# First spectral product in 64x64 blocks with the transform in quarters; behind the expert loop nested conditions, and the own rows of two images added by GpSimd

## The reference, cut to what matters

```python
o1r = relu(einsum(xr, w1[0]) - einsum(xi, w1[1]) + b1[0])   # per block of 24 channels
o1i = relu(einsum(xi, w1[0]) + einsum(xr, w1[1]) + b1[1])
o2r = softshrink(einsum(o1r, w2[0]) - einsum(o1i, w2[1]) + b2[0])
o2i = softshrink(einsum(o1i, w2[0]) + einsum(o1r, w2[1]) + b2[1])
x = irfft2(o2r + 1j * o2i) + x
t = t + attention(layernorm(t))
n = layernorm(t)
t = t + shared(n) + sum over two experts e of comb[:, e] * expert_e(n)
```

## Time and profile before

| | |
|---|---|
| median of 3 runs | 228.53 us |
| the profiled execution's own time | 227.28 us |
| its span, first to last instruction | 225.4 us |
| TensorE matmuls busy | 217.2 us (96%) |
| TensorE weight loads | 140.8 us (62%) |
| VectorE | 148.7 us (66%) |
| ScalarE | 113.8 us (50%) |
| GpSimd | 77.2 us (34%) |

### The profile page before, as it was taken

How to read it: one execution, slowest core, us unless ns; L and a number is a source line. 1 busy time by engine, 2 the same in 40 slices (tenths; PEclk the granted TensorE clock), 3 DMA queues, 4 the chain that set the end, 5 groups by cost and what they waited for, 6 DMA issues and landing times.

```text
span 225.4 us, 5766 instructions
## 1 busy us (share of the span) xinstructions
PE 217.2 (96%) x1975; PEld 140.8 (62%) x1975; DVE 148.7 (66%) x353; ACT 113.8 (50%) x205; POOL 77.2 (34%) x119
## 2 busy tenths in 40 slices
PE   7999999999999999999999999999999999897994
PEld 3988866765676676767755745655556565453393
DVE  3558767677878888787879756666566666560262
ACT  0742274555444444345643567566575766653271
POOL 7040052000001811837101626566565666442100
PEclk9999999999999999999999999999999999999999
DMA  6973564939989979015600211111211111210444
GB/s 179 184 186 88 153 237 102 292 75 354 287 165 292 244 200 286 0 38 171 198 20 0 52 34 52 52 42 52 52 52 48 52 40 52 55 35 22 146 153 140
DMA packets 28115, 27.53 MB, mean 122 GB/s; under 512 B 7804, under 2 KB 26940, under 8 KB 28092
## 3 DMA queue, kind: packets, MB, share of 16 engines
q1 hardware_dynamic: 22444, 21.15, 34.0%
q0 software_dynamic: 2304, 4.72, 7.5%
q10 hardware_dynamic: 3344, 1.36, 2.3%
HBM read 22.34 MB, written 3.44 MB: 114 GB/s over the span
## 4 chain that ended last, share of the span: by engine, by line
PE 88%; DVE 5%; ACT 3%; issue 2%
PE grid L1624 11%; PE bank L1650 10%; PE grid L1365 8%; PE grid L1631 7%; PE bank L1640 4%; PE bank L1385 4%; PE bank L1227 4%; PE grid L1511 3%; PE grid L1335 3%; PE bank L1402 3%; PE bank L1335 2%; PE bank L1287 2%; PE bank L1350 2%; PE grid L1525 2%; PE bank L1193 2%
## 5 line engine op out<-in xcount | busy, mean ns | idle before, releaser
L1110 DVE COPY main<-main 128x1152 f32 x39 | 30.3, 790 | 15.2 <-issue 13.6
L776 ACT ACTIVATE main<-down_all 128x576 f32 x40 | 27.2, 684 | 25.6 <-PE bank L1650 24.7
L742 ACT ACTIVATE main<-grid 128x1024 f32<-128x1024 f32 x23 | 23.6, 1025 | 26.3 <-PE grid L1365 26.3
L589 POOL DMA_INDIRECT main<-xhat_rows,main x21 | 26.9, 1282 | 24.4 <-PE bank L1610 13.4
L597 POOL DMA_INDIRECT pair_rows<-main x19 | 20.2, 1061 | 25.6 <-DVE main L1100 25.6
L1624 PE MATMUL grid<-main 128*64 128x384 f32 x152 | 28.2, 488 | 0.6 <-DVE main L1094 0.6
L1335 PE MATMUL grid<-main 32*128 32x256 f32 x132 | 27.1, 401 | 0.0
L1365 PE MATMUL grid<-main 32*128 32x256 f32 x192 | 26.3, 398 | 0.8 <-ACT main L742 0.6
L913 DVE TENSOR_REDUCE main<-grid 128x2 f32<-128x512 f32 x33 | 21.8, 685 | 4.4 <-PE grid L1335 3.6
L1650 PEld LDWEIGHTS bank<-main 128*64 128x64 f32 x228 | 16.1, 136 | 12.4 <-ACT main L776 8.9
L1650 PE MATMUL bank<-main 128*64 128x192 f32 x228 | 22.7, 333 | 0.0
(11 more groups left out here) (221 smaller groups left out, 395.3 us busy)
## 6 DMA issues: line engine op xcount, KB each, us to landing
down_all<-wd SPq DMA_DIRECT2D x4, 1152.0 KB, 7.0
main<-wg SPq DMA_DIRECT2D x4, 576.0 KB, 4.6
main<-wu SPq DMA_DIRECT2D x4, 576.0 KB, 6.1
main<-wg SPq DMA_DIRECT2D x4, 288.0 KB, 6.8
main<-wu SPq DMA_DIRECT2D x4, 288.0 KB, 8.0
main<-main SPq DMA_DIRECT2D x8, 128.0 KB, 3.6
main<-x SPq DMA_DIRECT2D x1, 768.0 KB, 7.5
main<-wg SPq DMA_DIRECT2D x2, 384.0 KB, 5.7
```

The source lines that it names most:

```text
L589: pool.indirect_dma_start(xg[:, t % 2, :], None, xhat_rows, bass.IndirectOffsetOnAxis(ap=slot_token[:, t:t + 1].bitcast(U32), axis=0)).the ...
L742: act.activation(probs[:, quad % 2, 2 * (n % 2):2 * (n % 2) + 2, :, :].rearrange("p h k n -> p h (k n)"), grid[:, score_banks(n), :], ACT. ...
L776: act.activation(w_dn[:, p, h, :], dn_e(expert(t, h)), ACT.Copy).then_inc(S["w_dn_ready"], 1)
L1110: vec.tensor_copy(w_gu[:, p, h, :], gu_e(expert(t, h))).then_inc(S["w_gu_ready"], 1)
```

## The change

It has three parts.

1. *The start.* `spec`, `hid`, `w1` and `w2` get a new layout of the 128 partitions: quarters of 32, real and imaginary part of one block of 24 channels, then of another. The transform (L1179) has 16 matmuls a unit with 32 output columns in place of 8 with 64. The first layer has 16 matmuls of 64x64 weights in place of 8 of 128x128, in steps of four that lie on the four quadrants of the array and go to two banks. Its evictions are shared: ScalarE takes one of the two banks (relu with bias), VectorE the other (add the bias, then the maximum with 0), counted by the new semaphore `hid_dve`; a step of the second pair of images waits for the evictions of the same step of the first pair. VectorE negates in two instructions of 32 partitions, that of `w2` in front of its third eviction. All of `w2` is loaded by SyncE, `b1` by four loads of ScalarE in place of two, and `w_proj` with its bias before `w_qkv`, the gate's loads (new semaphore `ld_gate`) behind it. The spreading to `w_first` stands behind L993.
2. *The loop.* `loop_pairs` reads the number of pairs before the loop. Pairs 8 to 11 stand unrolled, each in a condition inside the body of the one before.
3. *The tail.* For tiles 0 to 3 GpSimd adds the own rows to the first share, between `first_share` and `mix` (new semaphore `own_ready`). TensorE no longer transposes own rows of images 0 and 1. It does both parts of `shared_down` first, then the routed rows of all images, then the own rows of images 2 and 3. VectorE mixes two tiles in place of three before the last hidden product.

```diff
@@ -321,17 +322,20 @@
+            pairs = engine.value_load(used_i[0:1, 1:2], min_val=SURE // 2, max_val=TILES // 2)
...
-            pairs = engine.value_load(used_i[0:1, 1:2], min_val=SURE // 2, max_val=TILES // 2)
-            with engine.Fori(SURE // 2, PAIRS - 1) as i:
+            def further(i):
                 with engine.If(pairs > i):
                     step(2 * i, 0, i)
                     step(2 * i + 1, 1, i)
-            with engine.If(pairs > PAIRS - 1):
-                for t in range(TILES - 3, TILES - 1):
-                    step(t, t % 2, t // 2)
+                    if i + 1 < PAIRS:
+                        further(i + 1)
+            further(SURE // 2)
...
@@ -410,14 +414,21 @@
-        def load_blocks(queue, dst, src, sem, k):
-            i, o = slice(BLK * k, BLK * k + BLK), slice(BLK * k, BLK * k + BLK)
-            im = slice(IM + BLK * k, IM + BLK * k + BLK)
-            block_k = src.rearrange("r (q k) i o -> k r i q o", k=2)[k]
+        def load_w1(queue, k):
+            block_k = a["w1"].rearrange("r (k q) i o -> k r i q o", k=2)[k]
...
-                queue.dma_start(dst[i, :, r, o], block_k[r]).then_inc(sem, 16)
-                queue.dma_start(dst[im, :, 1 - r, o], block_k[r]).then_inc(sem, 16)
+                for imag in range(2):
+                    first = 64 * k + 32 * imag
+                    queue.dma_start(w1[first:first + BLK, :, r ^ imag, 0:BLK], block_k[r]).then_inc(S["ld_w1"], 16)
+        def load_w2(queue, s):
+            block_s = a["w2"].rearrange("r (g s) i o -> s r i g o", s=2)[s]
+            for r in range(2):
+                for imag in range(2):
+                    first = 64 * s + 32 * imag
+                    queue.dma_start(w2[first:first + BLK, :, r ^ imag, BLK * s:BLK * s + BLK], block_s[r]).then_inc(S["ld_w2"], 16)
...
@@ -426,16 +437,22 @@
-            load_blocks(sp, w1, a["w1"], S["ld_w1"], 1)
-            load_blocks(sp, w2, a["w2"], S["ld_w2"], 1)
-            sp.dma_start(w2[GC:GC + 1, :, :, :], a["b2"].rearrange("r n o -> r (n o)").rearrange("r (q c) -> q r c", c=GC).unsqueeze(0)).then_inc(S["ld_w2"], 16)
+            load_w1(sp, 1)
+            for side in range(2):
+                load_w2(sp, side)
+            sp.dma_start(w2[BLK:BLK + 1, :, :, :], a["b2"].rearrange("r n o -> r (n o)").rearrange("r (q c) -> q r c", c=GC).unsqueeze(0)).then_inc(S["ld_w2"], 16)
...
+            sp.wait_ge(S["w_zeroed"], 6)
+            for r in range(4):
+                sp.dma_start(wproj[32 * r:32 * r + HD, :, :],
+                             a["w_proj"].rearrange("(j r d) n -> r d j n", r=4, d=HD)[r]).then_inc(S["ld_attn"], 16)
+            sp.dma_start(bproj[:, :], a["b_proj"].partition_broadcast(128)).then_inc(S["ld_attn"], 16)
...
@@ -628,27 +637,33 @@
+            pool.wait_ge(S["shared_ready"], 2)
+            for t in range(NT // 2):
+                pool.wait_ge(S["share_ready"], t + 1)
+                nc.gpsimd.tensor_tensor(y_back[:, t, 0, :], y_back[:, t, 0, :], tok_b[:, t, :], ALU.add).then_inc(S["own_ready"], 1)
...
-            act.wait_ge(S["zeroed"], 5)
-            load_blocks(act, w1, a["w1"], S["ld_w1"], 0)
+            act.wait_ge(S["zeroed"], 3)
+            load_w1(act, 0)
...
-                for r in range(2):
-                    act.dma_start(b1[IM * r:IM * r + GC, :], a["b1"][r].rearrange("n o -> (n o)").rearrange("(q p) -> p q", p=GC)).then_inc(S["ld_b1"], 16)
-            load_blocks(act, w2, a["w2"], S["ld_w2"], 0)
+                for side in range(2):
+                    for r in range(2):
+                        first = 64 * side + 32 * r
+                        act.dma_start(b1[first:first + BLK, :], a["b1"][r].rearrange("(g s) o -> s o g", s=2)[side]).then_inc(S["ld_b1"], 16)
...
-            act.wait_ge(S["ld_b1"], 2 * 16)
-            for v in range(2 * GROUPS):
-                bp, q = v // GROUPS, v % GROUPS
+            act.wait_ge(S["ld_b1"], 4 * 16)
+            for v in range(0, 2 * GROUPS, 2):
+                bp, q = v // GROUPS, v % GROUPS // 2
...
@@ -855,7 +870,8 @@
-                vec.tensor_scalar(w[IM:, :, 0, :], w[IM:, :, 0, :], -1.0, None, ALU.mult).then_inc(S["negated"], 1)
+                for first in (32, 96):
+                    vec.tensor_scalar(w[first:first + 32, :, 0, :], w[first:first + 32, :, 0, :], -1.0, None, ALU.mult).then_inc(S["negated"], 1)
...
@@ -865,7 +881,14 @@
-            negate(w2, "ld_w2", 9)
+            dve.wait_ge(S["ld_b1"], 4 * 16)
+            for v in range(1, 2 * GROUPS, 2):
+                bp, q = v // GROUPS, GROUPS // 2 + v % GROUPS // 2
+                if v == GROUPS + 1:
+                    negate(w2, "ld_w2", 9)
+                dve.wait_ge(S["hid_done"], v + 1)
+                vec.tensor_scalar(hid[:, q, bp * 2 * MODES:(bp + 1) * 2 * MODES], bank[4 + v % 4][:, 0:2 * MODES],
+                                  b1[:, q:q + 1], 0.0, ALU.add, ALU.max).then_inc(S["hid_dve"], 1)
...
@@ -989,8 +1007,13 @@
-                    dve.wait_ge(S["ld_attn"], 9 * 16)
+                    dve.wait_ge(S["ld_attn"], 6 * 16)
...
+                    dve.wait_ge(S["ld_qkv"], 16 * 12)
+                    dve.wait_ge(S["w_zeroed"], 6)
+                    for rows, m, part in ((slice(0, 128), 0, 0), (slice(0, 128), 1, 1), (slice(64, 128), 2, 0), (slice(0, 64), 2, 1)):
+                        vec.tensor_copy(w_first[rows, m, :].rearrange("p (x t) -> p x t", t=2)[:, :, 0],
+                                        w_d[rows, m, 0, part, :]).then_inc(S["w_spread"], 1)
...
@@ -1139,16 +1162,18 @@
+                if t < NT // 2:
+                    dve.wait_ge(S["own_ready"], t + 1)
...
-            for t in range(SHARES_AHEAD):
+            for t in range(MIXED_AHEAD):
...
-            for t in range(SHARES_AHEAD, NT):
+            for t in range(MIXED_AHEAD, NT):
...
@@ -1173,32 +1198,38 @@
-                        col = y * C + (2 * (u % 2) + q) * GC
...
-                        for r in range(2):
-                            last = mm(bank[u][IM * r:IM * r + IM, at_mode:at_mode + MODES // 2], folded[:, b, col:col + IM],
-                                      fwd[:, y, r, :], start=True, stop=True)
+                        for k in range(2):
+                            col = y * C + (4 * k + 2 * (u % 2) + q) * BLK
+                            for r in range(2):
+                                last = mm(bank[u][64 * k + 32 * r:64 * k + 32 * r + 32, at_mode:at_mode + MODES // 2], folded[:, b, col:col + 32],
+                                          fwd[:, y, r, :], start=True, stop=True)
...
-            pe.wait_ge(S["negated"], 1)
-            for v in range(2 * GROUPS):
-                bp, q = v // GROUPS, v % GROUPS
+            pe.wait_ge(S["negated"], 2)
+            for bp in range(2):
...
-                if v >= 4:
-                    pe.wait_ge(S["hid_ready"], v - 3)
-                else:
-                    pe.wait_ge(S["spec_dve" if v % 2 else "spec_act"], B // 2 + v // 2 + 1)
-                mm(bank[4 + v % 4][:, 0:2 * MODES], w1[:, q, :, :], spec[:, q, bp * 2 * MODES:(bp + 1) * 2 * MODES],
-                   start=True, stop=True).then_inc(S["hid_done"], 1)
-            pe.wait_ge(S["negated"], 2)
+                for v in range(2):
+                    if bp:
+                        pe.wait_ge(S["hid_ready"], v + 1)
+                        pe.wait_ge(S["hid_dve"], v + 1)
+                    else:
+                        pe.wait_ge(S["spec_act"], B // 2 + v + 1)
+                        pe.wait_ge(S["spec_dve"], B // 2 + v + 1)
+                    for k, side in ((0, 0), (1, 1), (0, 1), (1, 0)):
+                        last = mm(bank[4 + 2 * v + k][64 * side:64 * side + 64, 0:2 * MODES], w1[64 * k:64 * k + 64, 2 * v + side, :, :],
+                                  spec[64 * k:64 * k + 64, 2 * v + side, bp * 2 * MODES:(bp + 1) * 2 * MODES], start=True, stop=True)
+                        if (k, side) in ((0, 1), (1, 0)):
+                            last.then_inc(S["hid_done"], 1)
+            pe.wait_ge(S["negated"], 4)
...
-                pe.wait_ge(S["hid_ready"], GROUPS * (pair + 1))
+                pe.wait_ge(S["hid_ready"], GROUPS // 2 * (pair + 1))
+                pe.wait_ge(S["hid_dve"], GROUPS // 2 * (pair + 1))
...
@@ -1687,34 +1720,27 @@
-            def out_columns(b, rows_of, begins):
+            def out_columns(b, rows_of, begins, ends):
...
-                                  is_transpose=True, start=(begins and h == 0 and (k == 0 or b == B - 1)), stop=not begins, skip_group_check=True)
-                if not begins:
+                                  is_transpose=True, start=(begins and h == 0 and (k == 0 or b == B - 1)), stop=ends, skip_group_check=True)
+                if ends:
...
-            for b in range(B // 2):
-                out_columns(b, own, True)
-            pe.wait_ge(S["hid_s_ready"], FC + low.stop)
-            for u in range(NT // 4, NT // 2):
-                shared_down(u, low)
```

(40 more changed lines are left out.)

21 lines of the change are left out of this document (9 added, 12 removed).

## The result

The changed kernel takes **229.38 us** (median of 20 executions, 227.72 to 233.21), the kernel before 228.00 (20 executions, 227.04 to 228.73). The ratio is **1.0061, 95% interval 1.0043 to 1.0080**: slower by 0.6%, 1.4 us, where 3.0 us of gain were forecast. The ratio leaves out the four executions more than 1.5% above the fastest, and the profiled one (232.02) is among them, so its rows show more loss than the median has.

A forecast was written before the change was run, and what follows sets the result against it. TensorE's work, two gaps in it and the last matmul were taken as the bound. Start -0.95 and end -2.1 gave -3.05: 224.2 against the profiled 227.28, or 225.5 us on the median, own range 224.0 to 226.5.

The forecast's parts named there:

- the 4.4 us of the transform: Start: 256 quarter-tile matmuls at 15.4 ns plus 0.4 us would take 4.4 us against 4.37, so no change.
- the 1.61 us of gap: Behind the loop: two empty passes and the last test become one test, taking away 1.61 us of TensorE gap.
- The third rival: Behind the loop: leaving the nested conditions costs an instruction fetch, TensorE resumes at 203.8, time 226.4 to 227.2 us; chance 0.12.
- the wait until 12.1: Start: the second layer waits for the negation of `w2` until about 12.1 instead of 13.06, gaining 0.95 us.
- Gain 0.78: Loop: reading `pairs` before the loop takes TensorE's load from its end, gaining 0.78 us (0.6 to 0.8).
- before the loop the load lies beside a queued down product: Before the loop: TensorE's load of the count is hidden by a queued down product of 1.2 us.
- the 204.7 of the prediction: Behind the loop: tile 18's down product, waiting for ScalarE's eviction, starts at 204.7 instead of 206.45, 1.75 us earlier.
- TensorE loses the 8 matmuls on the own rows of two images, 1.01 us: Tail: 1.01 us less TensorE work; GpSimd adds four tiles instead, about 0.6 us each.
- + 0.7 (for mixes and rows): Tail: 0.7 us given back for mixes and rows in the sum of the end.
- -0.95: Start: second layer at 12.1 instead of 13.06, a gain of 0.95 us (0.7 to 1.4).
- -1.0 (jump with the wait for ScalarE): Behind the loop: -1.61 us of gap, with +0.6 of waiting for ScalarE.

The follow-up runs named there:

- experiment 4: Kernel before with the changed start alone, plus ten instead of eight warm-up matmuls (229.57 us) or waits behind the eight (229.84 us).
- experiment 2: Kernel before with the count read before the loop and conditions left by jumps past one pair of steps (225.65 us) or up to two (227.91 us).
- loop_only: Kernel before with the loop of the changed one alone (count read before the loop, nested conditions): 227.41 us, ratio 1.0015.
- no_start: Changed kernel with the start of the kernel before, so loop and tail of the change: 229.10 us, ratio 1.0016.
- near_tail: Kernel before with short jumps out of the conditions and the tail of the change, start as before: 226.11 us, ratio 0.9935.
- near_all: Changed kernel with only its long jump replaced by short jumps past one pair of steps each: 227.80 us, ratio 0.9989.
- start_shift: Kernel before with the changed start alone and seven waits for a reached semaphore behind each warm-up matmul: 229.84 us, ratio 1.0072.
- start_warm: Kernel before with the changed start alone and ten instead of eight warm-up matmuls: 229.57 us, ratio 1.0088.
- near_exit: Kernel before with the count read before the loop and conditions left by short jumps past one pair of steps each: 225.65 us, ratio 0.9942.
- mid_exit: Kernel before with the count read before the loop and conditions where one branch passes two unrolled pairs of steps: 227.91 us, ratio 1.0026.
- idle_gap: Kernel before with short jumps and 140 waits for a reached semaphore behind TensorE's last branch: 235.00 us (before: 228.13).

## Why the prediction was wrong

Two steps of the prediction failed, and the same mechanism is behind both: TensorE waits for its next instructions to be fetched. The first is the 4.4 us of the transform, a term with no room for such a wait. The second is the 1.61 us of gap that was to vanish behind the loop. The third rival, 0.12, had the fetch behind the loop, with 0.4 to 1.2 us of gain kept in the tail; no case had it in the transform.

**The start.** "If that holds with 72 moving columns, the 256 take 256 x 15.4 = 3.9 us plus the same 0.4": the pace held. At full clock four quarter tiles start every 62 ns (112 matmuls from 7.45 to 9.20), 15.6 ns a matmul. What failed is that the pace was taken as the only limit: the transform took 7.15 us (4.87 to 12.02) for the 4.4. A matmul brings a weight load, so 256 of them are 512 instructions, and a block of 256 lasts 128 x 15.6 ns = 2.0 us. The fetches show among the DMA queues (here of the changed kernel, window 7.5 to 10):

```profile
q8 instruction: 1, 0.02, 3.8%
```

3.8% of 16 engines and 2.5 us is 1.5 us for one block, from 7.70 on, and TensorE went on at 11.14, 3.4 us after it began. A block that is used up in 2.0 us cannot hide that. The earlier trace rows were read for the engine's pace only; the 13 packets of the earlier trace rows, 1.1 us each, stood beside them. The old transform's 128 matmuls, as many instructions as one block, took 4.2 us from the first start to the last, longer than that. The other four profiles of the quarters agree: 2.9 to 3.5 us from the packet's start to TensorE going on, and a stall of 1.48 to 1.82.

"Runtime: NRT & Kernel Launch" of the Trainium skill (Instruction fetch mechanics) has the block of 256 instructions, but says that crossing into the next is "mostly hidden", because instructions are issued more slowly than they are filled in. Here that fails: 1.48 to 1.82 us were not hidden.

The second term, "4.4" for the transform, was also too low by the clock: 76 of the 256 matmuls ran at the lower level, 30 ns each, until 7.1 us (8 of 128 before, until 5.2). The level is read from their duration, 327 ns for 226; the profile's clock column has 1.00 there. That is 1.1 us, and 1.63 are the stall. How much of the 1.1 would be won without the late clock is open: experiment 4 won 0.16, with two more warm-up matmuls in front. The product took 2.8 us (1.36 and 1.31 for two groups each, and 0.16 of waiting for VectorE) where 2.4 were forecast and 4.08 stood before. VectorE's negation of `w2` stood at 14.01, behind evictions that were late, not behind a landing, so that the wait until 12.1 was not put to the test.

**The loop.** "Gain 0.78": right, at its place. The delay falls from 3.0 to 2.2 us over the loop's end (192.95 against 189.92, 200.85 against 198.61). But "before the loop the load lies beside a queued down product" looked at TensorE only. Every engine reads the count. On ScalarE the read (0.27 us at 142.5) and its register work stand in front of an eviction that TensorE waits for, and the delay grows there from 2.6 to 3.0: 0.4 us given back.

```profile
143.23 0.50 ACT main L803
143.73 0.24 issue
143.97 1.20 PE bank L1683 x12
```

**Behind the loop.** "Behind the loop two empty passes and the last test become one test: 1.61 us of gap." The one test took 3.77 us where the third rival had said 3.1, and the piece of issue grew from 1.61 to 2.61: 1.0 us of loss for 1.61 of gain. TensorE resumed at 207.41, which without the 2.2 us of delay is 205.2, for the rival's 203.8. The argument against it, that three shorter jumps cost 1.61 us together, was wrong in kind: they cost little because their targets were at hand, as experiment 2 shows with 0.22 to 0.34 us against 3.2 and 3.8. The rest of the argument was sound: with short jumps TensorE waits for ScalarE as forecast, and the start at 204.44 hits the 204.7 of the prediction.

**The clock** was in no case. In the profiled execution it falls from 1.00 to 0.66 over the 5 us behind the gap, which costs 1.7 us ((2.71 - 1.72) + (1.81 - 1.12)). The same gap does not always do it: behind 2.64 us in `loop_only` and 2.60 in `no_start` the four matmuls of the profiled executions last 1.72 us, as behind the old gap of 1.61, and the clock stays.

**The tail.** "TensorE loses the 8 matmuls on the own rows of two images, 1.01 us", "+ 0.7 (for mixes and rows)": -0.3 expected, -0.4 in the profiled execution (+4.8 to +4.4), -0.6 with the tail alone. The adds last 0.60 us as forecast. But the chain that was summed was too short. Where the down product of step 18 starts later (207.22 in `no_start`) or earlier (204.69 in `near_tail`) than with the tail alone (206.39), the scatter (2.3 to 3.4 us) and the reading back (3.4 to 3.9) set the end, and the last hidden product stands behind them by its place in the queues.

The sum of the profiled execution at the last matmul: start +2.6, count read +0.4, loop's end -0.8, long jump +1.0, clock +1.6, tail -0.4: +4.4. Forecast was -0.95, 0, -0.78, -1.0 (jump with the wait for ScalarE), 0 and -0.3. The median is only 1.4 us above the kernel before: of the +4.4, the clock's 1.6 and the 0.7 of the second stall are not in every execution, and the three parts alone add up to +0.7.

**Left open.** Whether the quarters delay the first rise of the clock: with eight warm-up matmuls it came at 6.1 to 7.1 us in all four profiles with quarters, and by 5.3 in seven of ten with halves, but at 6.2 to 7.0 in the other three. That the short idle time lowers the clock in some executions and not in others is shown; what decides between them is not. Nor is it shown where the clock is low in the executions without a long gap behind the loop (5 of 12 in `near_all`, 6 of 10 in `start_shift`, 2 of 4 in `start_warm`). The loads and moved copies of the start were not tried by themselves; no wait for one of them ends last in a profile.

## What to carry to other kernels

Count instructions as well as columns. Where these small matmuls run side by side, a block of 256 instructions is gone in 2 us and its successor takes 3, so halving a tile to double the pace bought nothing here. Leave conditions by jumps over little code, with the rare cases in a rolled loop. An idle gap on TensorE can have a second price behind it, the lower clock, so look at the spread of the executions and not at the median alone. And where a tail hangs on a round trip through memory, work taken from TensorE turns into waiting.

## What the runs showed of the hardware

- A branch of TensorE: 68 ns not taken, 0.22 to 0.34 us past one pair of steps (`near_exit`), 3.2 us past two (`mid_exit`) and 3.8 past three (`loop_only`, the changed kernel). ScalarE's and VectorE's, with fewer instructions in a step, took 50 and 63 ns.
- Four 128x32 weight tiles with 72 moving columns start 15.6 ns apart on the mean at full clock, 30 at the lower level (the changed kernel).
- From the start of a packet on the instruction queue to TensorE going on: 2.9 to 3.5 us in five transforms, 3.1 at the long jump; the packet itself took 0.9 to 1.5 us.
- Idle time on TensorE behind the loop and the clock: 1.61 us, 1.00 behind it in the profile, and 12 of 97 executions of that kernel at 0.990 or 0.991 with 0.8 us lost; 2.4 to 3.0 us, 1.00 in some executions and 2.0 to 3.4 us lost in others (5 of 12 with 2.43, 3 with 2.64, 7 with 2.60, 5 with 2.97); 7.17 us, 0.50 in the one profiled, and all six executions low.
- Waits on TensorE for a reached semaphore go two to an instruction, and these come every 106 ns, though each shows 51 (`idle_gap`).
